# Weights of the later attention layers: split during the first two layers and kept in DRAM, instead of split at the layer borders

## The reference, cut to what matters

```python
x = x + L0(x, cond)   # attention, times a coherence per key, plus a field; Wout
x = x + L1(x, mask)   # masked attention; Wo; rms norm; gain and shift from cond
x = x + L2(x, t)      # rms norm; attention; Wo; rms norm; SwiGLU with 2048 hidden
x = x + L3(x)         # 4x4 quaternion mixing
```

## Time and profile before

| | us |
|---|---|
| median of 3 runs | 3061.34 (3058.72 to 3062.87) |
| the profiled execution's own time | 3061.82 |
| its span in the trace | 3060.1 |
| PE busy in the span | 2926.5 |
| DVE busy | 2042.9 |
| ACT busy | 1367.8 |
| POOL busy | 705.3 |

### The profile page before, as it was taken

The page is one execution under the profiler, slowest core; times in us unless marked ns, Lnnn a source line. Parts: engine busy times, 40 slices in busy tenths (PEclk is TensorE's granted clock), DMA queues, the critical chain, the costliest instruction groups (busy, mean ns, idle before and its releaser), DMA issues. The chain is left out here.

```text
span 3060.1 us, 69590 instructions
## 1 busy us (share of the span) xinstructions
PE 2926.5 (96%) x27253; PEld 2531.9 (83%) x27253; DVE 2042.9 (67%) x3640; ACT 1367.8 (45%) x2219; POOL 705.3 (23%) x562
## 2 busy tenths in 40 slices
PE   6999999998999999988999999599999999999997
PEld 5899999997888888877888888488888888888886
DVE  5777777776788888788877776454444454665554
ACT  3454444544666666555656665332222232222221
POOL 1122222222211111143322332122222221111111
PEclk7999999999999999989999999699999999999999
DMA  3432333344444444534443434521112141111101
GB/s 138 88 86 73 92 86 96 86 97 115 94 101 108 99 106 103 131 92 101 106 110 103 110 103 86 163 69 55 56 55 69 55 147 47 42 45 52 55 28 42
DMA packets 493850, 266.89 MB, mean 87 GB/s; under 512 B 410752, under 2 KB 468224, under 8 KB 493216
## 3 DMA queue, kind: packets, MB, share of 16 engines
q1 hardware_dynamic: 493728, 265.21, 32.9%
HBM read 122.53 MB, written 41.94 MB: 54 GB/s over the span
## 5 line engine op out<-in xcount | busy, mean ns | idle before, releaser
L885 ACT ACTIVATE att_shifted<-att_shifted,keep_lift 128x512 f32<-128x512 f32 x384 | 276.6, 720 | 357.5 <-DVE att_shifted L1034 353.0
L1030 DVE TENSOR_REDUCE att_top<-att_bank_s 128x4 f32<-128x512 f32 x384 | 264.4, 689 | 230.4 <-PE att_bank_s L720 227.7
L1622 DVE TENSOR_TENSOR mlp_act_t<-mlp_bank_u,mlp_sg 128x512 f32<-128x512 f32 x128 | 88.5, 692 | 455.3 <-ACT mlp_sg L1524 451.6
L1664 POOL TENSOR_TENSOR mlp_al<-mlp_act_t,mlp_ah 128x512 fp32r<-128x512 f32 x128 | 175.0, 1367 | 857.5 <-ACT mlp_ah L1530 857.5
L1524 ACT ACTIVATE mlp_sg<-mlp_bank_g 128x512 f32<-128x512 f32 x128 | 76.6, 598 | 630.8 <-PE mlp_bank_u L1437 630.7
L880 ACT ACTIVATE att_pq<-att_shifted 128x512 f16<-128x512 f32 x384 | 240.7, 627 | 160.1 <-DMA att_pt<-att_pq 154.2
L1038 DVE TENSOR_TENSOR att_pq<-att_shifted,att_pq 128x512 f16<-128x512 f32 x384 | 276.9, 721 | 14.0 <-ACT att_pq L880 13.7
L735 PEld LDWEIGHTS att_bank_o<-keep_v,att_pt 128*128 128x128 f16 x7680 | 221.8, 96 | 69.3 <-issue 24.0
L735 PE MATMUL att_bank_o<-keep_v,att_pt 128*128 128x34 bf16 x7680 | 256.1, 178 | 21.6 <-DVE att_of L1060 11.4
L1034 DVE TENSOR_TENSOR att_shifted<-att_bank_s,att_top 128x512 f32<-128x512 f32 x384 | 265.6, 692 | 16.4
L671 PE MATMUL att_bank_a<-att_oth,att_woh 128*128 128x256 f32 x768 | 233.7, 304 | 1.6 <-DVE att_otl L1074 1.5
(11 more groups left out here) (256 smaller groups left out, 8162.7 us busy)
## 6 DMA issues: line engine op xcount, KB each, us to landing
resid<-att_xres SPq DMA_DIRECT2D x47, 512.0 KB, 3.0
mlp_xf<-resid SPq DMA_DIRECT2D x32, 512.0 KB, 4.5
mlp_res<-resid SPq DMA_DIRECT2D x32, 512.0 KB, 4.7
att_xin<-resid SPq DMA_DIRECT2D x31, 512.0 KB, 3.7
att_xres<-resid SPq DMA_DIRECT2D x31, 512.0 KB, 4.2
att_xin<-in_x SPq DMA_DIRECT2D x16, 512.0 KB, 3.9
att_xres<-in_x SPq DMA_DIRECT2D x16, 512.0 KB, 3.7
mlp_yt<-resid SPq DMA_DIRECT2D x16, 512.0 KB, 7.0
```

The costliest lines, as they stand in the source:

```text
L885: nc.scalar.activation(shifted[:, u % 2], shifted[:, u % 2], ACT.Exp, bias=k["lift"][:, 0:1], scale=SCALE).then_inc(exp_done, 1)
L1030: nc.vector.reduce_max(top[:, u % 2, :], bank_s, AX_X).then_inc(top_ready, 1)
L1664: nc.gpsimd.tensor_tensor(al[:, c % 2, :], act_t[:, c % 2, :], f32(ah[:, c % 2, :]), ALU.subtract).then_inc(a_low, 1)
```

## The change

The weights of the second and third layer come as 16 pieces, `w_next`: each is one half of the output columns of a matrix, 512 KB. In the bodies that `piece_of` names (1 to 14, 16 and 29) one piece is loaded after the first transpose into `spare[0]`, copied to its high part by ACT in slot 8 (`high_piece`), subtracted by POOL as the last of its splits (`low_piece`), and both parts are stored to DRAM by SP at the body's end (`store_piece`). At a border SP fetches finished parts straight into `wh` and `wl`, 16 fetches of 512 KB in rows of 1 KB: the first halves of k and q at the end of body 14 (30), v after the transposes of units 0 and 2 of body 15 (31), the second halves of k and q after those of units 4 and 6, and o after that of unit 6 and at the end of body 16 (32). ACT and POOL do nothing for weights there. `values_first` now holds for nothing but the start, so v comes last in every body.

```diff
-        spare = [sb(f"spare{n}", [P, CH // 2 * E]) for n in range(5)]
+        spare = [sb(f"spare{n}", [P, CH // 2 * E]) for n in range(3)]
+        part_h, part_l = sb("part_h", [P, CH // 2 * E], F32R), sb("part_l", [P, CH // 2 * E], F32R)
...
-        LOAD_AT = {-2: {1: [("v", 0)], 2: [("v", 1)], 3: [("k", 0)], 4: [("k", 1)], 6: [("q", 0)]}, -1: {2: [("q", 1)], 6: [("o", 0)], 7: [("o", 1)]}, 0: {}}
-        HIGH_AT = {-2: {9: [("v", 0)], 10: [("v", 1)]}, -1: {3: [("k", 0)], 4: [("k", 1), ("q", 0)], 5: [("q", 1)]}, 0: {6: [("o", 0)], 7: [("o", 1)]}}
-        LOW_AT = {-2: {0: [("v", 0), ("v", 1)]}, -1: {0: [("k", 0), ("k", 1), ("q", 0), ("q", 1)]}, 0: {0: [("o", 0), ("o", 1)]}}
+        PIECES = [(n, m) for n, m in (("k", 0), ("q", 0), ("v", 0), ("v", 1), ("k", 1), ("q", 1), ("o", 0), ("o", 1))]
...
+                return {G - 3: 12, G - 2: 13, G: 14, 2 * G - 3: 15}.get(i)
+            return i - 1 if cur[0] == 0 else None
...
         def values_first(i):
-            return isinstance(i, int) and i % G >= G - 2
+            return isinstance(i, int) and i < 0
...
+            def load_piece(p):
+                if positive(p):
+                    sp.wait_ge(piece_low, p)
+                    sp.sem_inc(load_begun, 1)
+                d = w_next[bass.ds(p, 1)].rearrange("n p e -> (n p) e")
+                sp.dma_start(spare[0][:], d).then_inc(piece_loaded, 16)
+
+            def store_piece(p):
+                sp.wait_ge(piece_low, p + 1)
+                sp.sem_inc(load_begun, 1)
+                for t, part in ((split_h, part_h), (split_l, part_l)):
+                    sp.dma_start(t[bass.ds(p, 1)].rearrange("n p e -> (n p) e"), f32(part[:])).then_inc(piece_stored, 16)
+
+            def new_weight(layer, n, m):
+                p = len(PIECES) * (layer - 1) + PIECES.index((n, m))
+                for t, w in ((split_h, wh), (split_l, wl)):
+                    sp.dma_start(f32(columns(w[n], m)), t[p].rearrange("p (c e) -> p c e", c=CH)).then_inc(new_weights[n, m], 16)
...
+                    at = i - G * layer if isinstance(i, int) else None
+                    if at == -2 and u == UNITS:
+                        sp.wait_ge(piece_stored, 32 * len(PIECES) * layer)
+                        for n in "kq":
+                            last_use(layer, n, 0)
+                            new_weight(layer, n, 0)
+                    if at == -1 and u in (0, 2):
+                        if u == 0:
+                            last_use(layer, "v", 1)
+                        new_weight(layer, "v", u // 2)
+                    if at == -1 and u in (4, 6):
+                        last_use(layer, "q", 1)
+                        new_weight(layer, "kq"[(u - 4) // 2], 1)
+                    if at == 0 and u in (6, UNITS):
+                        last_use(layer, "o", 1)
+                        new_weight(layer, "o", u // UNITS)
...
+                nc.scalar.activation(part_h[:], spare[0][:], ACT.Copy).then_inc(piece_high, 1)
...
+                    if s == 8 and piece_of(i) is not None:
+                        high_piece(piece_of(i))
...
+                nc.gpsimd.tensor_tensor(part_l[:], spare[0][:], f32(part_h[:]), ALU.subtract).then_inc(piece_low, 1)
```

More of the change, by code:

```diff
@@ L348, in _, with attention @@
                 ws.low(dve, n)
[L351 removed]
+def attention(nc, hold, k, x_in, x_out, wh, wl, a, split_h, split_l):
+    w_next = a["w_next"]
     ALL = 3 * G
@@ L397, in attention, with piece_of, columns @@
         halves = [slice(0, CH // 2), slice(CH // 2, CH)]
[L398 to L406, removed]
-        LOAD_AT = {-2: {1: [("v", 0)], 2: [("v", 1)], 3: [("k", 0)], 4: [("k", 1)], 6: [("q", 0)]}, -1: {2: [("q", 1)], 6: [("o", 0)], 7: [("o", 1)]}, 0: {}}
-        HIGH_AT = {-2: {9: [("v", 0)], 10: [("v", 1)]}, -1: {3: [("k", 0)], 4: [("k", 1), ("q", 0)], 5: [("q", 1)]}, 0: {6: [("o", 0)], 7: [("o", 1)]}}
-        LOW_AT = {-2: {0: [("v", 0), ("v", 1)]}, -1: {0: [("k", 0), ("k", 1), ("q", 0), ("q", 1)]}, 0: {0: [("o", 0), ("o", 1)]}}
-        def swap(i):
-            if isinstance(i, int):
[L415 to L422, removed]
+        FIRST = 6
+        loads = [(a["L0_" + n][:, m * CH // 2 * E:(m + 1) * CH // 2 * E], flat3(wh[n][:, part]), flat3(wl[n][:, part]))
+                 for n in "cvo" for m, part in enumerate(halves)]
+        ws = Splitter(nc, hold, "att", loads, [t[:] for t in spare[:3]])
+        PIECES = [(n, m) for n, m in (("k", 0), ("q", 0), ("v", 0), ("v", 1), ("k", 1), ("q", 1), ("o", 0), ("o", 1))]
+        def piece_of(i):
+            if isinstance(i, int):
+                return {G - 3: 12, G - 2: 13, G: 14, 2 * G - 3: 15}.get(i)
+            return i - 1 if cur[0] == 0 else None
+        def columns(w, m):
+            return w[:, :, m * E // 2:(m + 1) * E // 2]
         bank_a = [bank("bank_a0"), bank("bank_a1")]
@@ L435, in attention @@
         load_begun, end_begun = sem("load_begun"), sem("end_begun")
+        piece_loaded, piece_high, piece_low, piece_stored = (sem("piece_" + n) for n in ("loaded", "high", "low", "stored"))
+        new_weights = {at: sem("new_w" + at[0] + str(at[1])) for at in PIECES}
         v_first, v_rest, v_second, v_split = sem("v_first"), sem("v_rest"), sem("v_second"), sem("v_split")
@@ L647, in body @@
                     turn_probs(i, u)
+                    if u == 0 and piece_of(i) is not None:
+                        load_piece(piece_of(i))
+                    swap(i, u)
                     if u == 1 and post(i):
@@ L661, in body @@
                     store(i - 1)
+                if piece_of(i) is not None:
+                    store_piece(piece_of(i))
+                swap(i, UNITS)
             iterate(sp, body)
@@ L680, in project @@
                         pe.wait_ge(a_free[bk], n)
[L681 to L685, removed]
+                    if isinstance(p, int) and p == 0 and m == 0 and kind in "cv":
+                        pe.wait_ge(ws.low_done, 2 * "cv".index(kind) + 2)
+                    if isinstance(p, int) and p > 0 and p % G == 0:
+                        for half in range(2) if kind == "v" else (m,):
+                            pe.wait_ge(new_weights[kind, half], 32 * lay(p))
                     if fill == (("c", 0) if lay(p) == 0 else ("v", 0) if values_first(body_of(p, fill)) else ("k", 0)):
@@ L1250, in body @@
                     low_x(i + 1)
-                for n in swaps(i, 0, LOW_AT) if swap(i) and swap(i)[1] > -2 else []:
-                    ws.low_on_pool(pool, n)
                 if post(i):
@@ L1256, in body @@
                     low_t(i + 1)
-                for n in swaps(i, 0, LOW_AT) if swap(i) and swap(i)[1] == -2 else []:
-                    ws.low_on_pool(pool, n)
+                if piece_of(i) is not None:
+                    low_piece(piece_of(i))
                 if pre(i):
@@ L1672, in build @@
     scratch = [nc.dram_tensor(f"resid{n}", (G, P, CH, T), F32, kind="Internal").ap() for n in range(4)]
+    split = [nc.dram_tensor(f"split_{n}", (16, P, CH // 2 * E), F32, kind="Internal").ap() for n in "hl"]
     with ExitStack() as ctx:
```

33 lines of the change are left out of this document (15 added, 18 removed).

## The result

| | before | after |
|---|---|---|
| median of 20 executions, us | 3060.99 (3053.84 to 3067.36) | 3054.96 (3051.7 to 3060.83) |
| ratio, 95% interval | | 0.9982 (0.9976 to 0.9988) |
| the profiled execution, us | 3061.82 | 3060.83 |
| its span, us | 3060.1 | 3059.1 |

A forecast was written before the change was run, and what follows sets the result against it. PE was held full in mid-layer, with idle time and lowered clock at the borders to win. 16.8 - 8.1 - 11.3 - 3.2 = -5.8 us from 3061.8 gave 3056 (own range 3048 to 3064; overall range 3039 to 3076).

The forecast's parts named there:

- A: First layer, bodies 1 to 14: POOL's piece subtraction holds DVE's small product, 1.2 us a body, +16.8 us.
- the upper bound of 1.4 us a body: First layer: the whole 2.38 us subtraction runs behind DVE's operation ending at 529.04, giving 20 us over 14 bodies.
- The rule of the Trainium skill: SBUF port pair: VectorE with both inputs in SBUF and GpSimd reading SBUF exclude each other for a whole instruction.
- B: First border, bodies 14 to 17: PE's 6.99 us wait and its clock loss go, body 16 loses 2.5; -8.1 us.
- C: Second border, bodies 30 to 32: 35.7 us of idle time and clock fall to 23.9, less 0.5; -11.3 us.
- The lengths named as signs: Bodies 30, 31 and 32 at the second border should be near 40.5, 50 and 41.5 us.
- The estimate from the Trainium skill: Second border: each further fetch in a row lasts 1.2 us, not 1.8, making the gain there 13 to 14 us.
- D: Bodies 46 and 47: with q ahead of v, the 1.5 us wait and 1.7 us of clock go; -3.2 us.
- R1: First layer: the pieces are hidden and cost 0 to 3 us, time 3039 to 3042; chance 0.15.
- R2: First layer: each body's 1.2 us wait lowers PE's clock, 24 us more, time 3080; chance 0.12.
- R3: Both borders: fetches pile up, transposes late, clock falls; gains 10 to 14 us less, time 3066 to 3070; chance 0.15.
- the signs: Expected marks in the changed kernel, among them ACT's waits for transposes longest in body 31; over 8 us landing refutes.

The follow-up runs named there:

- experiment 1: Changed kernel with ACT copying the piece in slot 11 instead of slot 8; median 3042.5 us, ratio 0.9938 to the kernel before.
- experiment 2: Changed kernel without POOL's subtractions of pieces, all loads, copies, stores and fetches kept; median 3040.8 us, ratio 0.9938 to the kernel before.
- experiment 3: Changed kernel with each piece's subtraction issued as two of 128x512, still slot 8; median 3040.5 us, ratio 0.9929 to the kernel before.
- Experiment 4: Changed kernel with five tiles instead of three for the first layer's splits at the start; median 3051.3 us, ratio 0.9967 to the kernel before.
- experiment 8: Kernel before the change, each POOL subtraction for a half matrix issued as two of 128x512; median 3053.1 us, ratio 0.9976 to the kernel before.
- experiment 5: Changed kernel with border fetches of q's second and o's first half behind unit 7's transpose, not unit 6's; median 3050.7 us, ratio 0.9967 to before.
- experiment 6: Changed kernel fetching only the high parts at the borders, 8 transfers instead of 16; median 3043.6 us, ratio 0.9934 to the kernel before.
- experiment 10: Changed kernel, piece in slot 11, five start tiles, q and o fetches behind unit 7, k's second half behind unit 3; 3029.4 us, ratio 0.9896 to before.
- experiment 9: Changed kernel with piece in slot 11, five start tiles, q and o fetches behind unit 7; median 3034.0 us, ratio 0.9905 to the kernel before.
- Experiment 7: Kernel before the change, with k and q filled ahead of v in bodies 46 and 47; median 3057.9 us, ratio 0.9991 to the kernel before.
- the second profile: Changed kernel unaltered, one more profiled execution; span 3054.4 us.

## Why the prediction was right in sum and wrong in three terms

**A, pieces in the first layer, +16.8: right.** Measured +16.0 (14.9 in bodies 1 to 13, 1.1 in body 14), one PE wait of 1.28 us in each, `of` named, L1089 at 1.32 us. Experiments 1, 2 and 3 show the cause from three sides: moved, left out or cut in two, it gives the time back. One slip without effect: the upper bound of 1.4 us a body does not follow from its terms, which give 529.04 + 2.38 + 0.51 - 530.65 = 1.3, so 18 us and not 20. The rule of the Trainium skill (SBUF — State Buffer, shared port pair) held for the instruction and its whole length, and the cut shows that it is per instruction.

**The start, +4.4 to +5.4: not in the sum.** The step that failed is one that I did not take: I costed what the diff adds to bodies, and not what the loss of two `spare` tiles does where the same tiles carry the first layer's weights. Experiment 4 gives it back.

**B, the first border, -8.1: measured 0 to -1.1.** The 6.99 us did go, and POOL had held it: experiment 8 only cuts POOL's subtractions in two, and it fell to 3.75. Two steps failed. The first is the count of waits for transposes. "The fetch of q's second half now stands in front of unit 7 where the load of o stood" kept one wait of 2.0 us in body 15, and body 16 was given another of 2.0. The two fetches of k with the store, behind unit 4, made a third. The three took 7.0 us in one profile and 6.1 in the other, and smaller waits for `of`, `xl` and `xres` grew by about 1. Idle time was to fall by 6.4 us (6.99 + 0.6 + 0.9, less 2.1) and fell by 2.3 and 3.2, body 14's piece taken off. The second is the clock: it was to give 1.7 us back (2.1 less 0.4 in body 16), but the lowered time stayed at 10.2 us in both profiles, and PE, now busy in nearly all of it, took 2.4 and 2.1 us more. So body 15 was 48.8 and 47.5 us for a predicted 44, body 16 41.0 and 40.5 for 38.

Experiments 5, 6 and 10 change the place or the number of fetches (10 together with the piece and the tiles of 9). Bodies 15 to 17 follow: 122.9 to 126.6 us in the six profiles with the fetches as made, 120.1, 118.1 and 118.8 with the edits (121.0 in the kernel of 9).

**C, the second border, -11.3: measured -18.4 and -18.6.** Right: the 10.7 us for `ql` and `quarter` went, the norms' waits stayed, body 30 was 40.8 for a predicted 40.5. Mis-sized: what stays of waits and clock in bodies 31 and 32. Of idle time 17.5 us were left standing (23.9 less 6.4 of clock), and 13.7 stayed in bodies 30 to 32: late transposes took about 4.5 us where 6.5 were charged, and the 2.4 us at body 32's start became 0.9. Of the clock I charged 1.4, 2.5 and 2.5 us; the profile has one drop, in body 31, for at most 1.7, and none in 30 and 32. Over bodies 29 to 33 idle time fell by 12.2 us for a forecast of 8.4, busy time by 6.2 for 3.4, and the 0.5 for body 33 did not come. Body 31 was 46.6 for 50, body 32 38.7 for 41.5. (The lengths named as signs add up to a gain of 13.0 us, the terms to 11.8.) No experiment separates at this border what came from POOL's work and what from k and q ahead of v, on which the wait for `ql` hung; experiment 8 shows 3.2 us for POOL's long operations alone. The pile of fetches itself was there: four landed 1.6 us apart at the first border (728.89 to 733.61) and 2.0 at the second (1332.81 to 1338.81), for which 1.8 was taken. The estimate from the Trainium skill (DMA: Bandwidth & Descriptors, anatomy of one DMA), 1.2 us for each, was too short; that section's fit is for transfers that GpSimd issues, and SP issued these. By it C was to be 13 to 14, nearer to what came, but for a reason that the landings don't bear out.

**D, -3.2: right in kind, too small.** Body 46 gave 2.1 us in both profiles, and from its end to the layer's last maximum body 47 gave 2.5 and 2.3, mainly since the wait for `ql` and the lowered stretch behind it are gone: 4.4 to 4.6 us, above the bound of 3.5. Experiment 7 has 2.1 and 1.8 us in the same places. Body 45 has nothing to do with it: a wait of 1.3 us for a transpose stands there in the profile of before, in the first of after and in that of experiment 7, and not in the second of after.

**Of the rivals,** R1 and R2 are out (43.57 us in each body, clock 1.00). R3 held in part at the first border, where late transposes and the clock took nearly all of B's gain, and not at the second. The text on the range does not fit them: 3039 to 3076 takes in all of R1 (3039 to 3042) and leaves R2 (3080) out. Of the signs, ACT's waits for transposes were not longest in body 31 (4.1 us) but in body 30 (4.8 us), with 4.5 in body 15. No transpose in body 15 or 31 landed over 8 us after its issue; the latest took 7.3 us.

**In sum,** for the second profile, which is nearer to the median: +16.0 (A) + 4.4 (start) - 1.1 (B) - 18.6 (C) - 4.4 (D) - 1.7 (body 45) - 0.3 (the rest) = -5.7, as the spans differ. Against the forecast of -5.8 the start was 4.4 us and B 7.0 us too dear, C 7.3 us, D 1.2 us and A 0.8 us too cheap, and body 45 gave 1.7 us by chance. In the first profile, the slowest of its kernel, the errors do not cancel: its span is 1.0 us below that of before. A came out by its mechanism, but that the total came out is luck: errors of 11 us one way met errors of about the same size the other way.

## What to carry to other kernels

Before work is spread over idle slots of GpSimd, find the slot in which no VectorE operation with inputs in SBUF stands between it and TensorE, or cut it into instructions as short as the slack: here 16 us hung on the slot, and a cut in two did as well as moving it.
A transfer put into an in-order queue is paid by the next urgent one behind it. Put it right behind the last transpose that PE needs, or where the issuing engine has nothing to do; moving two halves at each border gave 4.6 us by the ratio and 7.8 us by the profile.
When a change takes buffers away, follow every user of them, the start of the kernel too.

## What was not expected of the hardware

- A wait's length alone does not tell whether PE's clock falls. 2.37 us in body 15 of the kernel of experiment 3 left it at 1.00, 2.16 us at the same place in after was followed by 3.4 us at half, and 14 waits of 1.28 us, one each 43.6 us, did nothing.
- POOL's operation is lengthened too when DVE is first: 2.72 us for 128x1024 beside L1077, 2.38 us alone in slot 11.
- The two profiles of one kernel differ by 1.2 us at the first border and by 1.6 in bodies 45 and 46, through PE's waits for transposes and the clock behind them; body 0, bodies 1 to 13, 18 to 28 and 34 to 44 agree within 0.1 us.
